# Down-projections of the first MLP: pairs of units as block multiplications with seven products

## The chip, the cores and the metric

One core of one Trainium2 chip. The kernel is written at the level of engines and semaphores: TensorE (PE; its weight loads are PEld), VectorE (DVE), ScalarE (ACT), GpSimd (POOL) and SyncE (SP), which issues nearly all transfers. The metric is the device time of one execution in microseconds, the median of the runs; before the change it is 2037.12 us (three runs, 2036.31 to 2037.77).

## The reference

32 sequences of 64 tokens with 512 features go through two layers, each an attention block with two MLPs and then an adapter. Cut to one layer:

```python
attn = softmax(einsum('btd,bTd->btT', x @ Wq, x @ Wk) * scale)
attn_out = einsum('btT,bTd->btd', attn, x @ Wv) @ Wp + bp
cms_out = gelu(attn_out @ cW1 + cb1) @ cW2 + cb2 + target_embed      # first MLP, 512 -> 2048 -> 512
modifier = gelu(concat([attn_out, cms_out]) @ mW1 + mb1) @ mW2 + mb2  # second MLP, 1024 -> 2048 -> 512
x = clip(x + cms_out + modifier, 0, 1)
h = gelu(x @ W_down[role] + b_down[role])                             # adapter, 512 -> 256 -> 512
x = layernorm(x + h @ W_up[role] + b_up[role]) * gamma[role] + beta[role]
```

All in float32.

## The kernel before

The tokens are taken in two halves of 1024, and each half goes through the two layers: four passes. Within a pass tokens form two blocks (b = 0, 1) of TB = 512. A float32 multiplication is made of three fp32r matmuls: each operand is split into a high part (ScalarE copies or applies gelu and rounds) and a low part (VectorE subtracts), and `product` (L663 to L674, the matmul on L672) issues high x high, high x low, low x high for each pair of 128x128 weights and 128x512 tokens.

**Units.** The 2048 hidden features of an MLP are taken 256 at a time: NG = 8 units for the first MLP (u = 0 to 7) and 8 for the second (u = 8 to 15). The up-projection of a unit, except of units 0 and 8 ("plain"), is a block multiplication of 2x2 blocks with seven products P1 to P7 (`term`, `terms`). A term of the first MLP has 6 matmuls, one of the second 12. The combinations of weight blocks that this needs are made by POOL in `combine` (L602), four instructions a unit; ScalarE's and VectorE's `weight_part` make the high and the low part of each. The results are put together from PSUM by ScalarE (`copy_p1`, `copy_p5`, `copy_u2`) and VectorE (`make_z22`, `make_z12`), and ScalarE's `hidden` applies gelu twice, once into a rounded high part and once into a full value, from which VectorE's `hidden` subtracts. The four 128x512 hidden blocks of a unit are H00, H10, H01, H11.

**Down-projections.** The plain form, `down` (L862), is used for units 0 to 8 and 15: for each token block and each of 4 output banks (d_out, PSUM banks 2 to 5) two hidden chunks, 6 matmuls; VectorE's `add` (L1692) then adds each bank of 128x512 to the accumulator (the result stays in SBUF). Units 9 to 14 (FAST) use a block multiplication here as well, `fast_down` (L881): seven products of two outputs each, with a part of w2 (`split_part`, `low_part`, 128x256, in one of five slots of wdp) as weights, and with hidden blocks or their differences (`hidden_sum` makes the difference, `split_sum` and `low_sum` its parts) as tokens. It works on two double banks, d_a (banks 2, 3) and d_b (4, 5); `copy_down` (L1201) copies d_a into d_b once a unit, and `fast_add` (L1673) adds a double bank, 128x1024, to the accumulator six times. POOL's `combine_down` (L618) makes the combinations of w2, four instructions of 128x256 a unit.

**Order.** Each engine runs one written-out program; nothing is scheduled at run time. PE's `mlps` (L901) puts the down-projection of unit u-1 between the terms of unit u: for units 1 to 7 the order is P1, P5, P6, block 0 of `down`, P2, P7, block 1 of `down`, P4, P3. The waits of `fast_down` that the prediction speaks of are:

```python
if i in (P6, P2):
    pe.wait_ge(d_copied, f + 1)
else:
    pe.wait_ge(acc_done, {P5: a0 - (1 if fast(u - 1) else 2), P3: a0 + 1, P1: a0 + 2, P7: a0 + 3, P4: a0 + 4}[i])
```

**Loads.** SP loads for each unit the up weights (`load_w1`, 512 KB into w1c or 1 MB into w1m) as soon as the parts of the unit before are made, and the down weights (`load_w2`, 512 KB into w2). At the start of a pass the tokens of the pass are stored to DRAM (xmid) and read back 256 KB at a time (xp) for the residual. x12 is a pair of high and low parts of one token block, which the plain units 0 and 8 read; for the first MLP it lies in the region cop, which the second MLP's operands use later.

Of the kernel before, what the change touches and what calls it, by code (L numbers as in the profile page):

```python
# [12 lines left out]
P = 128  # L13
# [59 lines left out]
DOWNS = 8 * (UNITS - len(FAST)) + 7 * len(FAST)  # L73
ADDS = 8 * (UNITS - len(FAST)) + 6 * len(FAST)
PARTS = UNITS - len(FAST) + 7 * len(FAST)

# [5 lines left out]
def cond_seq_kernel(nc, x_in, fuse_in, c1_in, c2_in, m1_in, m2_in, down_in, up_in, roles_in, rows_in, bias_in, ids_in, out):  # L82
    with ExitStack() as ctx:
# [7 lines left out]
        xmid = nc.dram_tensor("xmid", (P, NB * KC * SEQ), F32, kind="Internal").ap()  # L91
        brows = nc.dram_tensor("brows", (LAYERS, 2, BROW), F32, kind="Internal").ap()
# [6 lines left out]
        w2 = at("w2", [P, MC * V], F32, XI + 8)  # L99
        comb = at("comb", [P, 4 * P], F32, XI + 12)  # L100
        xp = at("xp", [P, TB], F32, XI + 14)
# [11 lines left out]
        aop_raw = at("aop_raw", [P, 7, 2, 2, TB], F32, AO)  # L113
        cop_raw = at("cop_raw", [P, 7, 2, 2, TB], F32, CO)
# [34 lines left out]
        wdp = at("wdp", [P, W2_SLOTS, 2, 2 * P], F32R, WT + 16)  # L149
        comb2 = at("comb2", [P, 2, 2 * P], F32, WT + 26)  # L150
# [81 lines left out]
        s_done, s_half, ss_done, mx_done, sm_ready, ex_done = (sem(n) for n in ("s_done", "s_half", "ss_done", "mx_done", "sm_ready", "ex_done"))  # L232
        rs_done, ri_done, p_zeroed, p_ready = sem("rs_done"), sem("ri_done"), sem("p_zeroed"), sem("p_ready")
# [6 lines left out]
        x12_hi, x12_lo, x12_used = sem("x12_hi"), sem("x12_lo"), sem("x12_used")  # L240
        quad_done = sem("quad_done")

        w1_loaded, w2_loaded, xp_loaded = sem("w1_loaded"), sem("w2_loaded"), sem("xp_loaded")
# [44 lines left out]
        def fasts(p, u):  # L288

            return len(FAST) * p + min(max(u - FAST[0], 0), len(FAST))  # L290

        def dn_at(p, u):

            return DOWNS * p + 8 * u - (fasts(p, u) - len(FAST) * p)

        def acc_at(p, u):

            return ADDS * p + 8 * u - 2 * (fasts(p, u) - len(FAST) * p)

        def d_at(p, u):  # L300

            return PARTS * p + u + 6 * (fasts(p, u) - len(FAST) * p)

        def plain_downs(p, u):
            return UNITS * p + u - fasts(p, u)
# [13 lines left out]
        def part_turn(u, i):  # L319
            return 7 * (u - FAST[0]) + DOWN.index(i)  # L320

        def part(u, i):
            return wdp[:, part_turn(u, i) % W2_SLOTS, :, :]

        def w2_block(half, chunk):
            return w2[:, (2 - chunk) * V + (half - 1) * 2 * P:(2 - chunk) * V + half * 2 * P]

        def part_source(i):
            return {P5: comb2[:, 0, :], P3: comb2[:, 0, :], P6: comb2[:, 1, :], P1: w2_block(1, 1), P2: w2_block(1, 2),
                    P7: w2_block(2, 1), P4: w2_block(2, 2)}[i]  # L330
# [80 lines left out]
        def h_sum(i):  # L411
            return {P5: hs_raw[:, 0, LO, 1, :], P6: zt[:, 3, :], P7: t34_raw[:, 0, LO, :], P4: t34_raw[:, 1, LO, :]}[i]
# [4 lines left out]
        def _(sp):  # L417
# [56 lines left out]
            def one_pass(half, layer, where, after):  # L474
# [37 lines left out]
                for u in range(UNITS):  # L512
# [27 lines left out]
                    if u + 1 < UNITS:  # L540
                        load_w2(u + 1)
# [1464 lines left out]
```

## Time and profile before

| | us |
|---|---|
| median of three runs | 2037.12 |
| lowest, highest | 2036.31, 2037.77 |
| the profiled execution, its own time | 2037.42 |
| its span on the core | 2035.5 |
| PE busy | 2021.2 (99%) |
| VectorE busy | 1508.2 (74%) |
| ScalarE busy | 1021.5 (50%) |
| POOL busy | 370.0 (18%) |

The granted TensorE clock over the span is 0.999 of full speed. A pass takes about 490 us; the MLPs of the first run from about 111 to 510 us. Times of an instruction in the rows are its start and its length. Instructions of one engine overlap at their ends, so a sum over many of them goes by the distance of their starts. Rows of a timeline merge neighbours of one kind and give their number (x6). A "[0.74 <-PE ...]" behind a row is the idle time of the engine before it and what ended it.

### The profile page before, as it was taken

What the parts mean: (1) busy time and instruction counts of PE and PEld (TensorE: products, weight loads), DVE (VectorE), ACT (ScalarE), POOL (GpSimd) and SP (SyncE); (2) the same over time, 40 slices, a digit from 0 to 9 for tenths busy, and PEclk for the clock granted to TensorE, in tenths of its full rate; (3) what the DMA queues carried; (4) which work ended last, traced back from release to release, by engine and by line L of the source; (5) the groups of instructions that cost most, each with busy time, mean ns of one, the idle gap of its engine ahead of it and who ended that gap; (6) DMA issues with size and microseconds to landing.
All of it is one profiled execution on the core that took longest, in us unless ns stands there. A gap on an engine that the chain in (4) does not pass through costs nothing.

```text
span 2035.5 us, 27682 instructions
## 1 busy us (share of the span) xinstructions
PE 2021.2 (99%) x9500; PEld 1692.2 (83%) x9500; DVE 1508.2 (74%) x2321; ACT 1021.5 (50%) x1844; POOL 370.0 (18%) x415
## 2 busy tenths in 40 slices
PE   9999999999999999999999999999999999999998
PEld 7888888888888888888888888888888888888887
DVE  7576677888767667888867666888886766778887
ACT  5464454555356444555435444555544544445552
POOL 0011112321101102232110110223210111032321
PEclk9999999999999999999999999999999999999999
DMA  8411211213411111112460121122252021211143
GB/s 292 166 32 42 73 47 63 73 59 113 161 68 42 52 65 60 48 62 73 155 234 22 51 63 67 37 73 73 71 189 104 11 62 42 78 62 47 62 145 95
DMA packets 42377, 169.78 MB, mean 83 GB/s; under 512 B 5624, under 2 KB 9720, under 8 KB 34808
## 3 DMA queue, kind: packets, MB, share of 16 engines
q1 hardware_dynamic: 42096, 167.97, 23.8%
q8 instruction: 80, 1.31, 0.3%
q14 instruction: 57, 0.47, 0.1%
q10 hardware_dynamic: 144, 0.03, 0.0%
HBM read 146.97 MB, written 21.01 MB: 83 GB/s over the span
## 4 chain that ended last, share of the span: by engine, by line
PE 95%; DMA 2%; DVE 2%; SPq 0%; issue 0%; POOL 0%; ACT 0%; DVEq 0%; ACTq 0%
PE psum L672 88%; DMA gains<-roles_in 1%; PE psum L966 1%; PE psum L1003 1%; PE psum L747 1%; PE psum L769 1%; DVE yt L1908 0%; PE psum L770 0%; PE psum L749 0%; SPq L422 0%; DMA fraw<-fuse_in 0%; PE psum L979 0%; PE psum L991 0%; DVE stats L1889 0%; PE psum L1015 0%
## 5 line engine op out<-in xcount | busy, mean ns | idle before, releaser
L672 PE MATMUL psum<-hs,wd 128*128 128x512 f32 x1920 | 448.8, 389 | 0.5
L672 PEld LDWEIGHTS psum<-hs,wd 128*128 128x128 f32 x1920 | 360.1, 188 | 76.9 <-DVE acc L1703 2.2
L672 PE MATMUL psum<-cop,wsm 128*128 128x512 f32 x1416 | 354.7, 389 | 0.0
L672 PE MATMUL psum<-aop,wsm 128*128 128x512 f32 x1320 | 333.0, 389 | 0.0
L672 PEld LDWEIGHTS psum<-cop,wsm 128*128 128x128 f32 x1416 | 265.8, 188 | 55.2
L672 PE MATMUL psum<-aop,wsc 128*128 128x512 f32 x1320 | 311.3, 389 | 0.0
L672 PEld LDWEIGHTS psum<-aop,wsm 128*128 128x128 f32 x1320 | 247.8, 188 | 51.4
L672 PEld LDWEIGHTS psum<-aop,wsc 128*128 128x128 f32 x1320 | 247.5, 188 | 51.4
L1679 DVE TENSOR_TENSOR acc<-psum,acc 128x1024 f32<-128x1024 f32 x144 | 175.6, 1219 | 87.2 <-PE psum L672 87.1
L1703 DVE TENSOR_TENSOR acc<-psum,acc 128x512 f32<-128x512 f32 x256 | 167.9, 684 | 84.5 <-PE psum L672 84.4
L1430 DVE TENSOR_TENSOR hs<-hs_raw,hs 128x512 fp32r<-128x512 f32 x256 | 178.8, 706 | 43.5 <-ACT hs_raw L1243 43.5
L1242 ACT ACTIVATE hs<-psum,bias 128x512 fp32r<-128x512 f32 x120 | 82.1, 684 | 237.2 <-PE psum L672 237.1
L672 PE MATMUL psum<-hs,wdp 128*128 128x512 f32 x576 | 146.2, 389 | 0.0
L1242 ACT ACTIVATE hs<-zt,bias 128x512 fp32r<-128x512 f32 x112 | 81.0, 723 | 113.7 <-PE psum L672 71.7
L672 PEld LDWEIGHTS psum<-hs,wdp 128*128 128x128 f32 x576 | 108.1, 188 | 22.4
L1171 ACT ACTIVATE wsm<-w1m 128x512 fp32r<-128x512 f32 x156 | 96.1, 622 | 37.0 <-DMA w1m<-m_in 37.0
L1430 DVE TENSOR_TENSOR wsm<-w1m,wsm 128x512 fp32r<-128x512 f32 x156 | 110.3, 723 | 1.3 <-ACT wsm L1171 1.0
L672 PE MATMUL psum<-t,wdp 128*128 128x512 f32 x432 | 109.6, 389 | 0.0
L1685 DVE TENSOR_TENSOR zt<-psum,zt 128x512 f32<-128x512 f32 x56 | 38.7, 691 | 80.2 <-PE psum L672 80.2
L609 POOL TENSOR_TENSOR comb<-w1c 128x256 f32<-128x256 f32 x28 | 20.7, 738 | 416.2 <-DMA w1c<-c_in 416.2
L672 PEld LDWEIGHTS psum<-t,wdp 128*128 128x128 f32 x432 | 81.1, 188 | 16.8
L616 POOL TENSOR_TENSOR w1m<-w1m,comb 128x512 f32<-128x512 f32 x28 | 45.4, 1620 | 269.8 <-DVE wsm L1430 269.8
(193 smaller groups left out, 3072.9 us busy)
## 6 DMA issues: line engine op xcount, KB each, us to landing
w1m<-m_in SPq DMA_DIRECT2D x32, 1024.0 KB, 4.9
w1c<-c_in SPq DMA_DIRECT2D x32, 512.0 KB, 3.5
w<-c_in SPq DMA_DIRECT2D x32, 512.0 KB, 3.6
w<-m_in SPq DMA_DIRECT2D x32, 512.0 KB, 3.5
gains<-roles_in SPq DMA_DIRECT2D x30, 512.0 KB, 5.1
fw<-fused SPq DMA_DIRECT2D x6, 2048.0 KB, 10.3
fused<-fw SPq DMA_DIRECT2D x4, 2048.0 KB, 7.6
xmid<-x SPq DMA_DIRECT2D x4, 2048.0 KB, 6.8
```

The costliest lines, as they stand in the source:

```text
L609: nc.gpsimd.tensor_tensor(st, w_block(u, 1, 0), w_block(u, 1, 1), ALU.add).then_inc(w1_sums, 1)
L616: nc.gpsimd.tensor_tensor(w_block(u, 0, 1), w_block(u, 0, 1), st, ALU.subtract).then_inc(w1_sums, 1)
L672: mm = nc.tensor.matmul(out, lhs(a), rhs(b), start=(start and n == 0), stop=(stop and n == total - 1), skip_group_check=reopened)
L747: nc.tensor.matmul(out, tq[:, j // 2, HI, j % 2, i * P:(i + 1) * P], xs[:, :, j, tile], start=(j == 0), stop=False)
L769: nc.tensor.matmul(out, val[:, HI, v_cols], val[:, :, p_cols], start=True, stop=False)
L966: nc.tensor.matmul(out, tokens, wdn_flat[:, bass.ds(role * (2 * KC * BN) + (c * KC + k) * BN, BN)], start=(b == 0 and k == 0 and a == c), ...
L1171: nc.scalar.activation(slot(u, i)[:, HI, :], w_source(u, i), ACT.Copy).then_inc(s_hi[i], 1)
L1242: nc.scalar.activation(hs[:, b, HI, m, :], h_source(h, u), ACT.Gelu, bias=b1)
L1430: return nc.vector.tensor_tensor(out, a, hi.bitcast(F32), ALU.subtract)
L1679: nc.vector.tensor_tensor(dst, bank, dst, ALU.add).then_inc(acc_done, 1)
L1685: nc.vector.tensor_tensor(zt[:, 2, :], bank_b()[:, :], zt[:, 2, :], ALU.add).then_inc(z22_done, 1)
L1703: nc.vector.tensor_tensor(dst, d_out[o][:, :], dst, ALU.add).then_inc(acc_done, 1)
```

## The change

The down-projections of units 1 to 6 (PAIRED) are no longer plain. Two units at a time, (1, 2), (3, 4) and (5, 6), go through `fast_down`: each of the seven products sums over both units in PSUM, so that a pair has seven products of 12 matmuls, six adds of 128x1024 and one copy of d_a into d_b. P5, P3 and P1 are issued within the unit behind the pair and P6, P2, P7, P4 in the one behind that; for (5, 6) all are within unit 7. Units 1 and 2 each take one token block of unit 0's plain down-projection. Unit 7 stays plain.

- The parts of w2 of a pair (14) go through seven slots, wdc; there are two buffers for w2 (w2 and w2b, the second for odd paired units).
- The hidden blocks and sums of units 1, 2, 4 and 5 go to two new sets of places, pairs, over the region cop. x12 of the first MLP is therefore stored to DRAM (kept, 1 MB) at unit 1 and read back before unit 8's third quarter product.
- POOL makes eight combinations of 128x256 for each pair, those of (1, 2) behind unit 1's `combine`, the others within `combine` of units 5 and 7, ahead of its last instruction.
- ScalarE's and VectorE's orders for units 1 to 7 are written out anew, instruction by instruction.
- The waits of several semaphores of the softmax are put on one semaphore (soft_step), with the same instructions.

PE's order and waits:

```diff
+                    for v in us:
+                        pe.wait_ge(d_lo, part_at(p, v, i))
+                        if i in SPLIT:
+                            pe.wait_ge(ht_lo, 4 * so_far(DENSE, p, v) + SPLIT.index(i) + 1)
...
+                    if i in (P6, P2):
+                        pe.wait_ge(d_copied, so_far(COPIES, p, us[-1]) + 1)
                     else:
+                        pe.wait_ge(acc_done, {P5: a0 - (2 if behind(u) is None else 1), P3: a0 + 1, P1: a0 + 2, P7: a0 + 3, P4: a0 + down_turn(u, P7)}[i])
                     out = d_b if i in (P6, P7, P4) else d_a
                     first = i in (P5, P1)
                     for o in range(2):
+                        mm = product(out[:, o, :], [(lambda a, v=v: part(v, i)[:, a, o * P:(o + 1) * P],
+                                                     lambda c, v=v: h_operand(v, i, c), None) for v in us], first, True, not first)
                     mm.then_inc(dn_done, 1)
...
+                    if u in (1, 2):
+                        terms(p, u, P1, P5, P6)
+                        down(p, 0, u - 1, 0, 1)
+                        terms(p, u, P2, P7)
+                        down(p, 0, u - 1, 2, 3)
+                        terms(p, u, P4, P3)
+                    elif u in (3, 5):
+                        terms(p, u, P1, P5, P6, P2)
+                        fast_down(p, u - 1, P5)
+                        terms(p, u, P7)
+                        fast_down(p, u - 1, P3)
+                        terms(p, u, P4)
+                        fast_down(p, u - 1, P1)
+                        terms(p, u, P3)
+                    elif u in (4, 6):
+                        terms(p, u, P1, P5)
+                        fast_down(p, u - 2, P6)
+                        terms(p, u, P6)
+                        fast_down(p, u - 2, P2)
+                        terms(p, u, P2)
+                        fast_down(p, u - 2, P7)
+                        terms(p, u, P7)
+                        fast_down(p, u - 2, P4)
+                        terms(p, u, P4, P3)
+                    elif u == NG - 1:
+                        terms(p, u, P1, P5, P6)
+                        fast_down(p, u - 1, P5)
+                        terms(p, u, P2)
+                        fast_down(p, u - 1, P3)
+                        terms(p, u, P7)
+                        fast_down(p, u - 1, P1)
+                        terms(p, u, P4)
+                        fast_down(p, u - 1, P6, P2, P7)
+                        terms(p, u, P3)
+                        fast_down(p, u - 1, P4)
```

SP's loop, POOL's order and unit 8's weights on ScalarE:

```diff
+                            for i in range(7):
+                                sp.wait_ge(s_lo[i], units(p, u, i) + 1)
+                        if u + 1 == NG:
+                            sp.wait_ge(d_lo, d_at(p, u))
+                            load_w2(u)
                         load_w1(u + 1)
...
+                    if paired(u):
+                        if u in (4, 6):
+                            sp.wait_ge(d_lo, d_at(p, u - 1))
+                            for v in group(u):
+                                load_w2(v)
+                    elif u == 0:
+                        sp.wait_ge(d_lo, d_at(p, u + 1))
+                        load_w2(2)
+                        sp.wait_ge(x12_lo, 2 * p + 1)
+                        sp.dma_start(kept, x12_flat).then_inc(x12_stored, 16)
...
+                        if u == NG - 1:
+                            sp.wait_ge(dn_done, dn_at(p, u))
+                            sp.wait_ge(x12_stored, 16 * (p + 1))
+                            sp.dma_start(x12_flat, kept).then_inc(x12_back, 16)
...
+                        elif u in (5, 7):
+                            combine_first(p, u)
+                            pair_first(p, u - 1)
+                            combine_last(p, u)
+                            pair_last(p, u - 1)
...
                 if u == NG:
+                    act.wait_ge(dn_done, dn_at(p, NG - 2) + down_turn(NG - 2, {P6: P2, P7: P7, P2: P4, P4: P4}[i]) + 1)
```

VectorE's new list where the first pair is worked off (within units 3 and 4; the lists of ScalarE and of the other units are of the same kind):

```diff
+                hidden(p, 2, H00)
+                fast_add(p, 2, P5)
+                low_part(p, 1, P1)
+                low_part(p, 2, P1)
+                low_sum(p, 2, P7)
+                make_z22(p, 3)
+                hidden(p, 2, H11)
+                fast_add(p, 2, P3)
+                low_sum(p, 2, P6)
+                low_part(p, 1, P6)
...
+                hidden_sum(p, 3, P4)
+                low_sum(p, 3, P5)
+                fast_add(p, 2, P6)
+                low_sum(p, 3, P7)
+                low_part(p, 2, P7)
+                fast_add(p, 2, P2)
+                low_part(p, 1, P4)
+                low_part(p, 2, P4)
+                weight_part(p, 5, P5)
+                fast_add(p, 2, P7)
```

## Rows read from the trace of the kernel before

**Rows 1.** The page: busy time of the engines, and the chain that ended last.
```profile
PE 2021.2 (99%) x9500; PEld 1692.2 (83%) x9500; DVE 1508.2 (74%) x2321; ACT 1021.5 (50%) x1844; POOL 370.0 (18%) x415
...
PE 95%; DMA 2%; DVE 2%; SPq 0%; issue 0%; POOL 0%; ACT 0%; DVEq 0%; ACTq 0%
```

**Rows 2.** A unit of each MLP: length, busy PE, PEld, DVE, ACT, POOL; PEclk; DMA.
```profile
166.63:187.03 20.40, 20.40 (x91) 16.90 (x90) 13.07 (x23) 9.83 (x20) 3.06 (x4) 1.00 0.17 52
358.39:386.95 28.56, 28.56 (x127) 23.66 (x126) 23.59 (x35) 15.62 (x29) 8.44 (x8) 1.00 0.18 65
```

**Rows 3.** Waits of the weight loads behind VectorE's adds, whole span.
```profile
PEld psum L672 <- DVE acc L1703: 2.2, 4, 0.5
```

**Rows 4.** Timeline of PE over one unit of the first MLP.
```profile
187.03 5.60 PE L672 MATMUL psum<-hs,wd 128*128 128x512 f32 x24
192.47 2.88 PE L672 MATMUL psum<-aop,wsc 128*128 128x512 f32 x12
...
200.63 6.96 PE L672 MATMUL psum<-aop,wsc 128*128 128x512 f32 x30
207.43 5.60 PE L672 MATMUL psum<-hs,wd 128*128 128x512 f32 x24
```

**Rows 5.** Timeline of VectorE, back-to-back instructions of three sizes.
```profile
347.78 1.22 DVE L1679 TENSOR_TENSOR acc<-psum,acc 128x1024 f32<-128x1024 f32 x1 [0.74 <-PE psum L672]
348.92 0.68 DVE L1430 TENSOR_TENSOR wsm<-w1m,wsm 128x512 fp32r<-128x512 f32 x1
349.52 0.42 DVE L1430 TENSOR_TENSOR wdp<-comb,wdp 128x256 fp32r<-128x256 f32 x1
349.86 0.68 DVE L1430 TENSOR_TENSOR wsm<-comb,wsm 128x512 fp32r<-128x512 f32 x1
```

**Rows 6.** Timeline, second MLP: products between fast_down products, and an add.
```profile
333.91 1.52 PE L672 MATMUL psum<-hs,wdp 128*128 128x512 f32 x6
336.44 1.21 DVE L1679 TENSOR_TENSOR acc<-psum,acc 128x1024 f32<-128x1024 f32 x1
336.63 1.52 PE L672 MATMUL psum<-cop,wsm 128*128 128x512 f32 x6
337.77 1.32 PEld L672 LDWEIGHTS psum<-hs,wdp 128*128 128x128 f32 x6
337.99 1.52 PE L672 MATMUL psum<-hs,wdp 128*128 128x512 f32 x6
...
346.15 1.52 PE L672 MATMUL psum<-t,wdp 128*128 128x512 f32 x6
```

**Rows 7.** Timeline, end of the second MLP: an add and the load behind it.
```profile
503.45 2.49 DVE L1703 TENSOR_TENSOR acc<-psum,acc 128x512 f32<-128x512 f32 x4
504.20 5.35 PEld L672 LDWEIGHTS psum<-hs,wd 128*128 128x128 f32 x24 [0.55 <-DVE acc L1703]
```

**Rows 8.** Timeline of ScalarE: the copy of d_a into d_b.
```profile
339.55 1.01 ACT L1205 ACTIVATE psum<-psum 128x1024 f32<-128x1024 f32 x1 [0.24 <-PE psum L672]
```

**Rows 9.** Timeline, first MLP: the chain of a combined weight part; POOL's instructions.
```profile
177.03 0.85 POOL L613 TENSOR_TENSOR comb<-comb,w1c 128x256 f32<-128x256 f32 x1 [4.37 <-DVE wsc L1430]
177.97 0.42 ACT L1171 ACTIVATE wsc<-comb 128x256 fp32r<-128x256 f32 x1 [2.15 <-issue]
178.03 0.74 POOL L616 TENSOR_TENSOR w1c<-w1c,comb 128x256 f32<-128x256 f32 x1
178.42 0.63 DVE L1430 TENSOR_TENSOR wsc<-comb,wsc 128x256 fp32r<-128x256 f32 x1 [1.13 <-ACT wsc L1171]
```

**Rows 10.** Timeline, second MLP: VectorE beside a POOL instruction.
```profile
361.93 1.68 POOL L616 TENSOR_TENSOR w1m<-w1m,comb 128x512 f32<-128x512 f32 x1 [10.01 <-DVE wsm L1430]
362.36 1.86 DVE L1430 TENSOR_TENSOR wdp<-w,wdp 128x256 fp32r<-128x256 f32 x2
```

**Rows 11.** Transfers: KB each, median us from issue to landing.
```profile
w1m<-m_in SPq DMA_DIRECT2D x32, 1024.0 KB, 4.9
w<-c_in SPq DMA_DIRECT2D x32, 512.0 KB, 3.6
```

More of the change, by code:

```diff
@@ new lines, in part_at, with w2_block, w2_odd, w2_here @@
+        def part_at(p, u, i):
+            if paired(u):
+                return d_at(p, group(u)[1]) + 2 * down_turn(u, i) + (u % 2 == 0) + 1
+            return d_at(p, u) + down_turn(u, i) + 1
+        def w2_block(u, half, chunk):
+            return (w2b if w2_odd(u) else w2)[:, (2 - chunk) * V + (half - 1) * 2 * P:(2 - chunk) * V + half * 2 * P]
+        def w2_odd(u):
+            return paired(u) and u % 2 == 1
+        def w2_here(p, u):
+            loads = [v for v in range(u + 1) if w2_odd(v) == w2_odd(u)]
+            per_pass = sum(w2_odd(v) == w2_odd(u) for v in range(UNITS))
+            return w2b_loaded if w2_odd(u) else w2_loaded, 16 * (per_pass * p + len(loads))
@@ new lines, in pair_last @@
+            def pair_last(p, u):
+                for i in (P5, P3):
+                    for v in group(u):
+                        if part_used(p, v, i):
+                            pool.wait_ge(dn_done, part_used(p, v, i))
+                        pool.wait_ge(w2_sums, w2_sum(p, v, P6))
+                        if i == P5:
+                            nc.gpsimd.tensor_tensor(part_source(v, P5), part_source(v, P6), w2_block(v, 1, 1), ALU.add).then_inc(w2_sums, 1)
+                        else:
+                            nc.gpsimd.tensor_tensor(part_source(v, P3), w2_block(v, 1, 2), part_source(v, P6), ALU.subtract).then_inc(w2_sums, 1)
@@ L790, in block_products @@
                     pe.wait_ge(s_lo[PLAIN[m, k]], n + 1)
-                    if b == 0:
+                    if kind and which == 0 and b and k == 0:
+                        pe.wait_ge(x12_back, 16 * (p + 1))
+                    elif b == 0:
                         pe.wait_ge(op_lo[(P1, P2)[k]], 2 * p + which + 1)
@@ L866, in down @@
                         pe.wait_ge(acc_done, acc_at(p, u) + o + 1)
-                    elif fast(u - 1):
+                    elif behind(u) is not None:
                         pe.wait_ge(acc_done, acc_at(p, u) - (o < 2))
@@ L896, in fast_down @@
                     for o in range(2):
-                        mm = product(out[:, o, :], [(lambda a: part(u, i)[:, a, o * P:(o + 1) * P], lambda c: h_operand(i, c), None)],
-                                     first, True, not first)
+                        mm = product(out[:, o, :], [(lambda a, v=v: part(v, i)[:, a, o * P:(o + 1) * P],
+                                                     lambda c, v=v: h_operand(v, i, c), None) for v in us], first, True, not first)
                     mm.then_inc(dn_done, 1)
@@ L922, in mlps @@
                         terms(p, u, P2)
[L923 to L929 removed]
+                        down(p, u - 1, 1, 0, 1)
+                        terms(p, u, P7)
+                        down(p, u - 1, 1, 2, 3)
                         terms(p, u, P4, P3)
```

681 lines of the change are left out of this document (536 added, 145 removed).

## Prediction

> **What bounds the kernel.** I read the page first: PE is busy 99% of the span, and the chain that ended last is 95% PE, 88% of it on L672, the line through which every product goes; VectorE is next with 74% [rows 1]. Then the two stages of one pass: in the steady units of the first MLP and of the second, PE is busy for the whole of each stretch, 20.40 of 20.40 us and 28.56 of 28.56 us, at a granted clock of 1.00, while VectorE has 13.07 and 23.59 us and ScalarE 9.83 and 15.62 us [rows 2]. The list of waits of the weight loads has almost nothing: 2.2 us behind accumulator adds in 2035 us [rows 3]. So inside the MLPs the time is the number of matmuls times their pitch, and nothing else is late. The pitch: from 187.03 to 207.43 us PE issues one unit, 24+12+24+30 = 90 matmuls (the row left out is the second block's 24), in 20.40 us [rows 4], 0.2267 us each.
>
> **What is removed.** A plain down-projection is 8 outputs x 2 chunks x 3 products of parts = 48 matmuls a unit, 96 for two. A pair needs 7 products x 2 outputs x 2 units x 3 = 84. Three pairs a pass save 36, four passes 144: 144 x 0.2267 = **-32.6 us**, all of it on the path, if PE stays fed. The units become uneven: units 1 and 2 have 66 matmuls (15.0 us), 3 and 5 have 78 (17.7), 4 and 6 have 90 (20.4), 7 has 126 (28.6).
>
> **What VectorE gains.** Pitches of back-to-back instructions, from one stretch [rows 5]: 128x1024 add 347.78 to 348.92, 1.14 us; 128x512 0.60; 128x256 0.34. Per two units, before: 14 weight parts, 28 of 128x512 (16 adds, 4 z sums, 8 hidden parts) and 2 of 128x1024 come to 4.8+16.8+2.3 = 23.9 of 40.8 us. After: 28 of 128x256 (14 weight parts, 14 low parts), 26 of 128x512 (4 z, 6 hidden, 8 sums, 8 low sums) and 6 adds of 128x1024: 9.5+15.6+6.8 = 31.9 of 38.1 us. So VectorE goes from 59% to 84% by pitch, and stays under PE. I walked its new list between successive make_z12, which can't run before a unit's last product: 13.6 us of work for the 15.0 of unit 2, 15.7 of 17.7, 16.3 of 20.4, 13.5 of 17.7, 20.7 of 20.4, 19.8 of 28.6. Only unit 6 is full, and it follows on one with 4 us to spare. ScalarE adds 14 weight splits, 8 sum splits and a 1 us copy per pair and loses 2 gelus and 2 wide copies, by my count some 26 of 38.1 us; it has 9.83 of 20.40 now [rows 2]. I take the bulk of both as hidden behind PE.
>
> **What comes onto the path: short windows.** In a pair, P3 accumulates in the banks of P5 after those were read out, P1 overwrites them after the next add, and P4 accumulates after the add of P7 (the acc_done waits in fast_down). In the second MLP two products of the next unit, 12 matmuls or 2.72 us, stand between, as between those at 333.91 and 337.99, three times 1.36 us apart [rows 6]; there an add that started late, 336.44, was done at 337.65 for a weight load at 337.77 [rows 6]. In the first MLP a term has one half only: 6 matmuls, 1.36 us. An add starts 0.27 us after the next product's first matmul (the product at 346.15 is followed at 347.51, and its add starts at 347.78 [rows 5, 6]), takes 1.22 us, and a waiting weight load begins 0.06 us behind its end (four adds take 2.49 us at a pitch of 0.60, so one is 0.69 long: 503.45+0.69 = 504.14, then 504.20 [rows 7]). Without a wait the load leads its matmul by 0.22 us (337.77, 337.99 [rows 6]). So PE loses 0.27+1.22+0.06-(1.36-0.22) = 0.41 us at each such place. These are P5 to P3, P3 to P1 and P7 to P4 in each of three pairs: 9 x 0.41 = 3.7 us a pass. In unit 7 also P1 to P6, where ScalarE's copy of 1.01 us with 0.24 before it [rows 8] gives 0.24+1.01+0.06-1.14 = 0.17. Per place the bounds are 0 (completion seen earlier than the row tells) and 1.0 (VectorE busy with one more 128x512 instruction, 0.60, when the add could start); I take 0.41, since at the places I followed VectorE has all earlier work done some us before.
>
> **Smaller terms.** Unit 2's P6 weights hang on a chain that starts only with unit 1's last gelu: VectorE sum, weight part P5, POOL 0.85, ScalarE 0.42, VectorE 0.63 [rows 9]. From the gelu's start at 13.8 us of unit 1 I get 17.7 against a load due at 17.5: 0.2 us a pass, bounds 0 and 1. Units 3 to 7 get these parts earlier.
> POOL has 8 more instructions of 128x256 per pair, 0.74 us each [rows 9], and those for pairs 3/4 and 5/6 stand ahead of combine_last, so of the P3 weights of units 5 and 7: in unit 7 P3 comes next to last, 25 us in; covered. While POOL runs, VectorE instructions that read SBUF alone wait: two of 128x256 took 1.86 us instead of 0.76, and ended 0.61 us behind POOL's 361.93+1.68 [rows 10]. A unit of the second MLP loses 23.59-21.8 (its pitches added up) = 1.8 us of VectorE to 8.44 us of POOL [rows 2]; a pair has some 12 us of POOL, so 2.5 us out of 6.2 spare. Only the burst of POOL work at the end of unit 6, where weight parts P7 and P6 of unit 7 are behind it, may show: 0 to 1.5 us a pass, I take 0.3.
> SyncE's queue: load_w1 waits for all seven parts of a unit instead of P3 alone, and P3 or P4 is made last anyway. Keeping x12 in DRAM is a 1 MB store in unit 1 and a 1 MB load in unit 7/8; w1m, of that size, lands in 4.9 us [rows 11], each has over 7 us. load_w1 of unit 8 moves behind the last part of the pair, about 19 us into unit 7; with w2 (3.6 and 4.9 us [rows 11], one after the other at worst) it is there by 28, and the first product that needs it starts at 30. The P2 and P4 weights of unit 8 wait for the last product of the pair and have the 2.72 us of the first quarter product; ScalarE 0.24+2x0.62, VectorE 0.68: 2.2 us. Covered by some 0.3 us, cost 0; if missed, under 1 us a pass.
>
> **The sum.** The profiled execution took 2037.42 us (span 2035.5, 1.9 around it), 0.3 over the median of 2037.12. Per pass stalls of 3.7+0.2+0.2+0.3 = 4.4 us, in four passes 17.6. 2037.4-32.6+17.6 = 2022.4, against the median 2022.1. **Forecast 2022 us**, 0.7% less. What a measurement can tell from no change is about 0.2%, 4 us.
>
> **Rivals.**
> A, the windows cost nothing and nothing else does: 2037.1-32.6 = 2004.5; with half the stalls 2013. For it: no add in the second MLP ever held PE up. Against: there the window is 2.72 us, here half. Chance 0.15 for 2004 to 2014.
> B, VectorE's own queue becomes late as well: besides the 0.41 each add then waits for what stands ahead of it. With 2 us more in each of pairs 3/4 and 5/6: 4 x 4 = 16 us more, 2038, with half of it 2030. For it: 84% by pitch, unit 6 at 101%. Against: 76% by pitch (21.8 of 28.56) stalls nothing in the second MLP. Chance 0.17 for 2028 to 2041.
> C, slower: POOL and VectorE serialise. From make_z12 of unit 1 to that of unit 7, VectorE has 99.6 us of work for 119.8 us of PE; POOL has 40 instructions there x 0.74 = 29.6 us. If each blocked VectorE for its whole length, VectorE would need 129.2, 9.4 us a pass over PE: 2037.1-32.6+37.6 = 2042. It decides from 20 us of blocked time a pass. For it: the stretch at 361.93 [rows 10]. Against: the second MLP would need 21.8+8.4 = 30.2 us of its 28.56 by that, and doesn't stall [rows 2, 3], since many instructions read PSUM or fall into waits. Chance 0.05.
> The Trainium skill, page "SBUF — State Buffer", section "SBUF: two separate sides", calls the port pair of VectorE and GpSimd an exclusive lock that blocks the other for the whole instruction, also for VectorE instructions with two SBUF inputs; by that rule taken for all POOL time the outcome would be C's. In the stretch above the trace agrees with it; over a unit it costs a fifth of POOL's time.
> D, the change does not do what it says: with 96 matmuls a pair nothing would go, 2037. The loops of fast_down issue 84. Chance 0.01.
> That leaves 0.62 for the forecast, 2015 to 2028.
>
> **The numbers.** Range: B's nearer part and A's half-stall case go in, 2009 to 2031; outside are A's end, most of C and the far end of B, under 0.2 together. Faster by over 0.2% (below 2033): 0.62+0.15+0.13 = 0.90; within 0.2%: 0.04; slower: 0.06.
>
> **What would show it.** Some 140 fewer PE instructions than the 9500, hs,wd down from 1920 to 768 (six units x 48 x 4 gone), PE's pitch still 0.2267. Weight loads idle behind the adds of line fast_add: 36 waits of about 0.41 us, 15 us in all, four of 0.2 behind the d_b copy. VectorE busy about 24 us more per pass in the first MLP (8.0 a pair). Second MLP unchanged at 28.56 us a unit. Wrong would be: waits of the adds over 1 us (B), no such waits (A), VectorE without idle time across units 3 to 7 with long 128x256 instructions (C), or a new wait at unit 8 behind x12_back or the P2 and P4 weights.

## The result, and the profile after

| | before | after |
|---|---|---|
| median, us | 2037.07 (8 runs) | 2030.42 (8 runs) |
| lowest, highest | 2036.31, 2038.87 | 2027.78, 2031.98 |
| the profiled execution; its span | 2037.42; 2035.5 | 2027.78; 2026.0 |

The ratio is 0.9965, with a 95% interval of 0.9954 to 0.9976: 6.65 us faster. Forecast were 2022 us, 15 us faster, with a range of 2009 to 2031 that just holds the result. The profiled execution of after happens to be the quickest of its eight; between the two profiles the gain is 9.6 us. So of the 32.6 us of matmuls taken away, 26 came back as waiting by the medians and 23 by the profiles, where 17.6 were forecast.

The page of after, its first line, the chain and two groups; it answers to [rows 1]:

```profile
PE 2004.1 (99%) x9356; PEld 1660.4 (82%) x9356; DVE 1637.2 (81%) x2513; ACT 1102.4 (54%) x2072; POOL 474.7 (23%) x511
...
PE 88%; DVE 6%; DMA 2%; issue 2%; ACT 1%; POOL 1%; SPq 0%; DVEq 0%; ACTq 0%
...
L831 PE MATMUL psum<-hs,wd 128*128 128x512 f32 x768 | 181.2, 390 | 0.5
...
L734 POOL TENSOR_TENSOR comb<-w1c 128x256 f32<-128x256 f32 x28 | 23.8, 849 | 300.4 <-DMA w1c<-c_in 300.4
```

The 144 matmuls are gone (9500 to 9356), and hs,wd fell from 1920 to 768 as the change says. PE's share still reads 99%. What is new stands in the chain: VectorE had 2% of it and has 6%, "issue" has 2%. The last line is one of POOL's old instructions, which the change does not touch: 0.74 us before, 0.85 on average now.

The stretches of after: the MLPs of the first pass, and one unit of the second MLP [rows 2]. Columns: length, busy PE, PEld, DVE, ACT, POOL, then the clock and the DMA share.

```profile
110.63:502.20 391.57, 389.13 (x1700) 317.27 (x1698) 330.37 (x481) 226.28 (x425) 109.11 (x103) 1.00 0.20 69
...
358.20:386.76 28.56, 28.56 (x127) 23.65 (x126) 23.59 (x35) 15.62 (x29) 8.43 (x8) 1.00 0.20 65
```

and the same stretch of the kernel before in its first pass:

```profile
110.69:504.20 393.51, 393.39 (x1737) 325.46 (x1735) 298.57 (x433) 206.00 (x368) 82.05 (x79) 1.00 0.19 65
```

The pass gained 1.94 us where 36 matmuls of 0.2267 are worth 8.16, so 6.2 came back as waiting. The second MLP is as it was, 28.56 us a unit and no wait at unit 8, and the clock is 1.00. All that came back lies in units 1 to 7 of the first MLP. POOL is busy 27.1 us more a pass for 24 new instructions (17.8 us at 0.74 each), VectorE 31.8 more where I had forecast 24.

The waits of the weight loads in after, whole span:

```profile
PEld psum L831 <- issue: 19.8, 45, 1.0
PEld psum L831 <- DVE wsc L1787: 10.2, 16, 1.0
PEld psum L831 <- DVE wdc L1787: 5.2, 8, 1.1
...
PEld psum L831 <- DVE acc L2063: 2.2, 4, 0.5
```

Against [rows 3], where only the last of these stood with 2.2 us, there are three new ones. The timeline of PEld over units 1 to 7 of the first pass says where they are; these are its rows with a wait, less eight more windows like the one at 163.03, of 0.44 to 0.51, and one wait of 0.17 at 236.97. The other three passes have the same waits at the same places, to about 0.1 us; only the one at 205.98 is missing in the second pass.

```profile
130.62 1.23 PEld L831 LDWEIGHTS psum<-aop,wsc 128*128 128x128 f32 x6 [1.04 <-DVE wsc L1787]
138.97 1.23 PEld L831 LDWEIGHTS psum<-aop,wsc 128*128 128x128 f32 x6 [0.31 <-DVE wsc L1787]
140.95 1.23 PEld L831 LDWEIGHTS psum<-aop,wsc 128*128 128x128 f32 x6 [0.76 <-DVE wsc L1787]
163.03 2.59 PEld L831 LDWEIGHTS psum<-pairs,wdc 128*128 128x128 f32 x12 [0.44 <-issue]
...
198.64 0.53 PEld L831 LDWEIGHTS psum<-hs,wdc 128*128 128x128 f32 x3 [1.13 <-DVE wdc L1787]
...
205.98 1.22 PEld L831 LDWEIGHTS psum<-aop,wsc 128*128 128x128 f32 x6 [0.38 <-issue]
...
235.58 1.23 PEld L831 LDWEIGHTS psum<-aop,wsc 128*128 128x128 f32 x6 [0.53 <-DVE wsc L1787]
...
249.88 0.53 PEld L831 LDWEIGHTS psum<-pairs,wdc 128*128 128x128 f32 x3 [0.22 <-issue]
```

Read them in three kinds. **The windows**: nine of 0.44 to 0.51, all at the places named in the prediction. **The copy site**: 249.88, 0.22. **The rest**: P7 of unit 1 (1.04), P5 and P6 of unit 2 (0.31, 0.76), P5 of pair 3/4 (1.13), P4 of unit 5 (0.38), P6 of unit 7 (0.53), P5 of pair 5/6 (0.17), together 4.3 us of waits a pass. For that third kind I had forecast 0.5.

A window is labelled "issue", which names nobody; the timeline of after around the first of them shows who ends it:

```profile
161.49 1.52 PE L831 MATMUL psum<-aop,wsc 128*128 128x512 f32 x6
163.06 2.98 PE L831 MATMUL psum<-pairs,wdc 128*128 128x512 f32 x12
165.88 1.52 PE L831 MATMUL psum<-aop,wsc 128*128 128x512 f32 x6
...
161.69 1.23 DVE L2039 TENSOR_TENSOR acc<-psum,acc 128x1024 f32<-128x1024 f32 x1 [1.16 <-PE psum L831]
```

The add starts 0.20 us behind the next product's first matmul, ends at 162.92, and the load follows at 163.03. VectorE stood idle 1.16 us before it, so nothing but the width of the window holds PE up. The loss is smaller than the wait. The load that waited leads its matmul by 0.03 us (163.03, 163.06) where 0.22 is usual [rows 6], so the matmul comes only 0.21 late (161.49+1.36 = 162.85 would be in time); the twelve matmuls from there take 2.82 us instead of 2.72. From 161.49 to 165.88 PE took 4.39 us for 18 matmuls, which are 4.08 at the pitch: 0.31 a window. At a wait of the third kind it is alike: around the one of 1.04, from the product at 128.49 to the one at 132.12, PE took 3.63 us for 12 matmuls, which are 2.72, so it lost 0.91.

The third kind has another face. VectorE and POOL in after, ahead of the wait at 198.64 (VectorE's rows first):

```profile
174.07 0.68 DVE L2050 TENSOR_TENSOR zt<-psum,zt 128x512 f32<-128x512 f32 x1
...
188.36 1.23 DVE L1787 TENSOR_TENSOR hs<-hs_raw,hs 128x512 fp32r<-128x512 f32 x1
189.51 1.83 DVE L1787 TENSOR_TENSOR wsc<-w1c,wsc 128x256 fp32r<-128x256 f32 x2
191.27 0.41 DVE L1787 TENSOR_TENSOR wsc<-comb,wsc 128x256 fp32r<-128x256 f32 x1
...
191.94 1.82 DVE L2023 TENSOR_TENSOR pairs_raw<-pairs_raw 128x512 f32<-128x512 f32 x2
193.87 1.04 DVE L1787 TENSOR_TENSOR pairs<-pairs_raw,pairs 128x512 fp32r<-128x512 f32 x1
194.83 1.23 DVE L2023 TENSOR_TENSOR pairs_raw<-pairs_raw 128x512 f32<-128x512 f32 x1
195.98 0.68 DVE L2050 TENSOR_TENSOR zt<-psum,zt 128x512 f32<-128x512 f32 x1
...
196.91 1.21 DVE L2039 TENSOR_TENSOR acc<-psum,acc 128x1024 f32<-128x1024 f32 x1
198.05 0.41 DVE L1787 TENSOR_TENSOR wdc<-wdc_raw,wdc 128x256 fp32r<-128x256 f32 x1
...
193.17 1.19 POOL L777 TENSOR_TENSOR wdc_raw<-comb2p,w2b 128x256 f32<-128x256 f32 x1
...
195.47 1.18 POOL L779 TENSOR_TENSOR wdc_raw<-w2b,comb2p 128x256 f32<-128x256 f32 x1
```

VectorE has no more than 0.11 us of idle time from 188.36 to the part at 198.05 for which PE waits, and many of its instructions are stretched: a 128x512 of SBUF operands takes 1.04 to 1.23 us instead of 0.68, two of 128x256 take 1.83 instead of 0.76. POOL's take 1.18 instead of 0.74. Beside each other both are slower. Where POOL stands idle, from 191.07 to 192.10, VectorE's 128x256 at 191.27 has its usual 0.41. L2050 is make_z12: of unit 3 at 174.07, of unit 4 at 195.98.

### The profile page after: what moved, and what is told of

Read it like the earlier page. It is cut to its first block, busy times and chain, and to the rows that moved or that the text cites. A ratio compares the mean times of both kernels' runs of the same rounds, so it can differ in the third digit from the quotient of the medians.

```text
span 2026.0 us, 28718 instructions
## 1 busy us (share of the span) xinstructions
PE 2004.1 (99%) x9356; PEld 1660.4 (82%) x9356; DVE 1637.2 (81%) x2513; ACT 1102.4 (54%) x2072; POOL 474.7 (23%) x511
## 4 chain that ended last, share of the span: by engine, by line
PE 88%; DVE 6%; DMA 2%; issue 2%; ACT 1%; POOL 1%; SPq 0%; DVEq 0%; ACTq 0%
PE psum L831 81%; PE psum L1161 1%; DVE wsc L1787 1%; PE psum L1198 1%; DMA gains<-roles_in 1%; PE psum L906 1%; PE psum L928 1%; DVE pairs_raw L2023 1%; DMA w1c<-c_in 1%; DVE yt L2455 0%; PE psum L1174 0%; DVE acc L2039 0%; PE psum L929 0%; PE psum L908 0%; DMA fraw<-fuse_in 0%
## 5 line engine op out<-in xcount | busy, mean ns | idle before, releaser
L2039 DVE TENSOR_TENSOR acc<-psum,acc 128x1024 f32<-128x1024 f32 x216 | 263.5, 1220 | 116.3 <-PE psum L831 115.5
L831 PE MATMUL psum<-aop,wsc 128*128 128x512 f32 x1320 | 320.7, 391 | 4.2 <-DVE wsc L1787 4.0
L831 PEld LDWEIGHTS psum<-aop,wsc 128*128 128x128 f32 x1320 | 246.0, 188 | 61.6 <-DVE wsc L1787 10.2
L831 PE MATMUL psum<-hs,wd 128*128 128x512 f32 x768 | 181.2, 390 | 0.5
L831 PE MATMUL psum<-pairs,wdc 128*128 128x512 f32 x672 | 177.6, 393 | 1.2
L831 PEld LDWEIGHTS psum<-hs,wd 128*128 128x128 f32 x768 | 143.8, 188 | 32.1 <-DVE acc L2063 2.2
L831 PEld LDWEIGHTS psum<-pairs,wdc 128*128 128x128 f32 x672 | 123.6, 188 | 36.4 <-issue 11.5
L1787 DVE TENSOR_TENSOR hs<-hs_raw,hs 128x512 fp32r<-128x512 f32 x192 | 135.5, 718 | 9.7 <-ACT hs_raw L1447 9.7
L1446 ACT ACTIVATE hs<-psum,bias 128x512 fp32r<-128x512 f32 x80 | 54.8, 685 | 76.4 <-PE psum L831 76.4
L831 PE MATMUL psum<-fw,xs 128*128 128x512 f32 x384 | 93.1, 395 | 0.0
```

The lines of the kernel that those rows point to most:

```text
L831: mm = nc.tensor.matmul(out, lhs(a), rhs(b), start=(start and n == 0), stop=(stop and n == total - 1), skip_group_check=reopened)
L1446: nc.scalar.activation(h_high(u, h), h_source(h, u), ACT.Gelu, bias=b1)
L1787: return nc.vector.tensor_tensor(out, a, hi.bitcast(F32), ALU.subtract)
L2039: nc.vector.tensor_tensor(dst, bank, dst, ALU.add).then_inc(acc_done, 1)
```

## The experiments

Two theories stood after this reading. **P**: POOL's new instructions hold VectorE up, and its lateness makes the third kind. **W**: the short windows are the larger part. Each has its own kernel. All ratios below are to the kernel before as it was measured beside each run (its medians lie from 2036.61 to 2037.48 us), with 95% intervals. That of after is 0.9954 to 0.9976; a kernel is told apart from after only where its interval lies clear of this one.

**e1_halves**: the windows. The adds of the pairs are made as two of 128x512, and P3, P1 and P4 wait for each bank by itself.

```diff
+                        if paired(u) and i in (P3, P1, P4):
+                            k = {P3: 1, P1: 2, P4: 5}[i]
+                            if o == 0:
+                                pe.wait_ge(acc_half, 18 * p + 6 * (us[-1] // 2 - 1) + k)
+                            else:
+                                pe.wait_ge(acc_done, a0 + k)
...
+                if paired(u):
+                    nc.vector.tensor_tensor(dst[:, 0, :], bank[:, 0, :], dst[:, 0, :], ALU.add).then_inc(acc_half, 1)
+                    nc.vector.tensor_tensor(dst[:, 1, :], bank[:, 1, :], dst[:, 1, :], ALU.add).then_inc(acc_done, 1)
+                    return
                 nc.vector.tensor_tensor(dst, bank, dst, ALU.add).then_inc(acc_done, 1)
```

> The changed kernel, with each of the pairs' adds of 128x1024 made as two of 128x512, and P3, P1 and P4 of a pair waiting for the add of their own bank only. Theory W (short windows): with half an add the wait for the first bank ends 0.27+0.69+0.06 = 1.02 us behind the product, before the weight load is due at 1.14, so the nine weight-load waits of 0.44 us a pass vanish and each gives back the 0.31 us that the matmuls lose now: 36 x 0.31 = 11 us, to about 2019; VectorE pays 18 x 0.06 = 1.1 us a pass. Rival L (VectorE is what is late, and the windows only show it): the same time turns up at other waits behind VectorE, gain under 3 us, 2028 to 2031.

Measured: 2027.38 us (2025.3 to 2031.1), ratio 0.9958 (0.9945 to 0.9972), span 2023.5. All nine windows are gone, but the time fell by only 3 us against after, and the two intervals overlap, so that even these 3 us are not settled. That is what rival L had said, not theory W. Its timeline of PEld and of VectorE at the place where after waited 1.13 us:

```profile
198.60 0.53 PEld L832 LDWEIGHTS psum<-hs,wdc 128*128 128x128 f32 x3 [1.98 <-DVE wdc L1794]
...
198.01 0.41 DVE L1794 TENSOR_TENSOR wdc<-wdc_raw,wdc 128x256 fp32r<-128x256 f32 x1
```

The load starts at 198.60, in after at 198.64. PE got there 0.85 us sooner and waited 0.85 us longer: here VectorE sets the time, and the three windows ahead of it were worth nothing. P4 of unit 5 went from 0.38 to 0.76 and P6 of unit 7 from 0.53 to 0.96 likewise.

**e2_thin_pool**: POOL. The 24 new instructions of POOL a pass are 16 columns wide and off the data; w2 of units 1 to 6 goes uncombined, so the sums of these units are not the reference's, and everything else is as in after.

```diff
-            if paired(u) and i in (P5, P3):
-                return wdc_raw[:, part_turn(u, i) % PAIR_SLOTS, LO, :]
+            if paired(u) and i in (P5, P3, P6):
+                return w2_block(u, *{P5: (2, 1), P3: (1, 2), P6: (2, 2)}[i])
...
-                    nc.gpsimd.tensor_tensor(w2_block(v, 2, 1), w2_block(v, 1, 1), w2_block(v, 2, 1), ALU.subtract).then_inc(w2_sums, 1)
+                    nc.gpsimd.tensor_tensor(comb2p[:, 1 - v % 2, 0:16], w2_block(v, 1, 1)[:, 0:16], w2_block(v, 2, 1)[:, 0:16], ALU.subtract).then_inc(w2_sums, 1)
```

> The changed kernel, with the 24 POOL instructions a pass that combine w2 for the pairs cut from 256 to 16 columns and taken off the data (the parts are split from uncombined w2 blocks, so the combinations of w2 of units 1 to 6 are left out); counts, waits and order are as before. Theory P (VectorE and POOL hold each other up through their shared access to SBUF): the 0.95 to 1.23 us instructions of VectorE at units 1, 4, 5 and 6 return to 0.42 and 0.68, and the waits at P7 of unit 1 (1.04), P5 of pair 3/4 (1.13), P4 of unit 5 (0.38), P6 of unit 7 and P5 of pair 5/6 (0.53+0.17) go or shrink below 0.2: about 2.5 to 3 us a pass, 2018 to 2021. Rival O (the order of the instruction lists makes them late, whatever POOL does): these waits stay within 0.2 us each, time within 3 us of the changed kernel's 2030.

Measured: 2020.21 us (2018.74 to 2021.33), ratio 0.9918 (0.9904 to 0.9931), span 2018.4: 10 us less than after by the medians, 7.6 by the spans. The waits of its weight loads, whole span, and VectorE in the stretch shown above:

```profile
PEld psum L831 <- issue: 19.8, 46, 1.0
...
PEld psum L831 <- DVE wsc L1787: 3.4, 8, 0.5
```

```profile
189.54 0.42 DVE L1787 TENSOR_TENSOR wsc<-w1c,wsc 128x256 fp32r<-128x256 f32 x1
190.89 1.49 DVE L2023 TENSOR_TENSOR pairs_raw<-pairs_raw 128x512 f32<-128x512 f32 x2 [0.94 <-ACT pairs_raw L1447]
192.48 0.69 DVE L1787 TENSOR_TENSOR pairs<-pairs_raw,pairs 128x512 fp32r<-128x512 f32 x1
```

VectorE has its usual lengths and even idles 0.94 us; P5 of pair 3/4 and P6 of unit 7 wait for nothing, of the waits behind wsc a third is left, of those behind wdc none. P4 of unit 5 waits 0.20 instead of 0.38. P7 of unit 1 still waits 0.53 and P6 of unit 2 0.32, more than theory P had left them. The windows are untouched. e2 also takes away that the parts have to wait for POOL's results; but ahead of the waits at 130.62, 198.64 and 235.58 VectorE in after runs on without idle time, so it was not waiting for a result there. P is right. W, that the windows are the larger part, is not: singly they are worth 3 us against 10.

**e6_thin_halves**: both edits together. Do they add?

> The two runs before taken together: adds of the pairs in halves, and the pairs' POOL instructions of 16 columns off the data (w2 of units 1 to 6 is not combined). Singly they gave 3 us and 10 us against the changed kernel's 2030.4. Theory S (two costs that cover each other: the waits at the windows give a late VectorE time to catch up, so taking them away pays in full only when VectorE is on time): now the windows pay their whole 36 x 0.31 = 11 us, and the time is 2020.2-11 = 2009, 21 us under the changed kernel. Rival (they add as measured singly): 2017.

Measured: 2010.87 us (2010.4 to 2012.58), ratio 0.9866 (0.9851 to 0.9881), span 2010.8. The windows are worth 9.3 us here against 3 without e2's edit, near theory S (2009) and far from its rival (2017): two losses that cover each other, since a PE that waits in a window lets a late VectorE catch up. All that waits in units 1 to 7 of its first pass now:

```profile
130.03 1.23 PEld L832 LDWEIGHTS psum<-aop,wsc 128*128 128x128 f32 x6 [0.53 <-DVE wsc L1794]
139.93 1.23 PEld L832 LDWEIGHTS psum<-aop,wsc 128*128 128x128 f32 x6 [0.48 <-DVE wsc L1794]
202.88 1.23 PEld L832 LDWEIGHTS psum<-aop,wsc 128*128 128x128 f32 x6 [0.49 <-issue]
245.13 0.53 PEld L832 LDWEIGHTS psum<-pairs,wdc 128*128 128x128 f32 x3 [0.22 <-DVE wdc L1794]
```

1.72 us a pass, 6.9 in four; by the spans 32.6-(2035.5-2010.8) = 7.9 us are still missing. The two agree within 1 us, so the matmuls are worth what was said.

**e3_units12**: only the order around units 1 and 2. POOL holds pair 1/2's combinations back until the parts of unit 1 are made and makes the last four in unit 2; the P5 part of unit 2 goes ahead of a hidden block on ScalarE and ahead of a hidden difference on VectorE.

```diff
+                            pool.wait_ge(s_lo[P7], UNITS * p + 2)
                             pair_first(p, u)
+                        elif u == 2:
+                            combine(p, u)
                             pair_last(p, u)
...
+                weight_part(p, 2, P5)
                 hidden_sum(p, 1, P5)
-                weight_part(p, 2, P5)
```

> The changed kernel, with the order alone changed at units 1 and 2: POOL waits for unit 1's P7 part before it combines w2 for pair 1/2 and does the second half of that after unit 2's combinations; ScalarE and VectorE make unit 2's P5 part before the gelu of H10 and the hidden difference. Theory: P7 of unit 1 (weight load 1.04 us late) loses 0.5 to 0.9 us less, P5 and P6 of unit 2 (0.31 and 0.76) are on time: 1.6 to 1.9 us a pass, 6 to 8 us in all, 2022 to 2024. Rival: the chain only moves, P6 of unit 2 stays late by over 0.5 us, gain under 3 us.

Measured: 2035.16 us, ratio 0.9993 (0.9984 to 1.0002), 5 us slower than after. Its first waits:

```profile
129.95 1.23 PEld L834 LDWEIGHTS psum<-aop,wsc 128*128 128x128 f32 x6 [0.50 <-DVE wsc L1790]
140.33 1.22 PEld L834 LDWEIGHTS psum<-aop,wsc 128*128 128x128 f32 x6 [0.99 <-DVE wsc L1790]
159.39 2.57 PEld L834 LDWEIGHTS psum<-pairs,wdc 128*128 128x128 f32 x12 [1.46 <-issue]
```

P7 of unit 1 went from 1.04 to 0.50, as wanted; P6 of unit 2 rose from 0.76 to 0.99, and P5 of pair 1/2, which had waited for nothing, waits 1.46. Part of the waiting was moved and none of it saved: the three places have 2.95 us of waits together, after had 2.11 in this stretch. The rival had said that the chain only moves; that the kernel gets slower neither had said.

**e4_units57**: three exchanges in VectorE's list, at P5 of pair 3/4, P4 of unit 5 and P6 of unit 7.

```diff
                 low_part(p, 3, P5)
+                low_part(p, 4, P5)
                 fast_add(p, 2, P4)
-                low_part(p, 4, P5)
...
+                make_z22(p, 5)
                 low_part(p, 4, P1)
-                make_z22(p, 5)
...
+                weight_part(p, 7, P6)
                 hidden_sum(p, 6, P5)
-                weight_part(p, 7, P7)
                 hidden_sum(p, 6, P6)
-                weight_part(p, 7, P6)
                 low_sum(p, 6, P5)
                 low_part(p, 5, P5)
                 low_part(p, 6, P5)
+                weight_part(p, 7, P7)
```

> The changed kernel, with VectorE's order alone changed at three places: the P5 part of unit 4 ahead of the add of pair 1/2's P4, make_z22 of unit 5 ahead of unit 4's P1 part, and unit 7's P6 part ahead of unit 6's differences with its P7 part behind the pair's parts. Theory: the waits at P5 of pair 3/4 (1.13 us) and at P4 of unit 5 (0.38) vanish, those at unit 7 (0.53+0.17) shrink to 0.3: 1.6 to 1.9 us a pass, 6 to 8 us, 2022 to 2024. Rival (VectorE has no room there, each instruction moved up makes another late): the sum of the waits behind VectorE in units 5 to 7 stays above 1.8 us a pass, gain under 3 us.

Measured: 2033.68 us, ratio 0.9985 (0.9976 to 0.9994), 3 us slower than after by the medians.

```profile
198.09 0.53 PEld L831 LDWEIGHTS psum<-hs,wdc 128*128 128x128 f32 x3 [0.56 <-DVE wdc L1787]
202.84 0.53 PEld L831 LDWEIGHTS psum<-hs,wdc 128*128 128x128 f32 x3 [0.79 <-issue]
...
236.04 1.22 PEld L831 LDWEIGHTS psum<-aop,wsc 128*128 128x128 f32 x6 [1.41 <-issue]
```

and PE and ScalarE at the last of these places:

```profile
236.07 1.63 PE L831 MATMUL psum<-aop,wsc 128*128 128x512 f32 x6 [1.01 <-ACT psum L1408]
...
234.20 0.63 ACT L1394 ACTIVATE hs<-hs_raw 128x512 fp32r<-128x512 f32 x1 [2.19 <-DVE hs_raw L2023]
```

P5 of pair 3/4 fell from 1.13 to 0.56, the window behind it grew from 0.44 to 0.79, P4 of unit 5 stopped waiting, and P6 of unit 7 rose from 0.53 to 1.41. The third exchange was aimed at the wrong instruction. VectorE's P6 part is now done at 233.02, but PE waits there for ScalarE's copy_p1 (L1408) as well, whose copy ends at 235.93, 0.11 ahead of the load; and ScalarE had stood idle 2.19 us for VectorE's difference (L2023), which stands behind the part now and ends at 234.16. In after the difference was done at 233.70 and the copy at 235.47, next to the part's 235.51, so that moving the part alone could gain nothing. In e3 and e4 the rival was right that little is to be gained, but both kernels came out slower than after (e4 only just clear of its interval), which neither side had said.

**e7_dve_sums**, **e8_dve_sums_halves**: is it the sharing itself, or has VectorE too much to do? The 24 combinations a pass are moved from POOL to VectorE, at about the places where POOL made them (0.42 us each there); e8 has e1's halves as well.

```diff
-                            pair_first(p, u)
-                            pair_last(p, u)
...
                 make_z22(p, 4)
+                pair_sum(p, 3, P7)
+                pair_sum(p, 4, P7)
                 low_sum(p, 3, P4)
                 hidden(p, 3, H00)
+                pair_sum(p, 3, P6)
+                pair_sum(p, 4, P6)
```

> The changed kernel, complete, with the eight combinations of w2 of each pair made by VectorE instead of POOL, each of 128x256 at a pitch of 0.34 us, put into its list at units 1, 2, 4 and 6. Theory P (it is POOL's hold on VectorE's access, 0.74 us a POOL instruction, that makes VectorE late): 24 x 0.34 = 8 us more work a pass for VectorE and yet no instruction of 0.95 to 1.23 us at units 4 and 6, and the waits there shrink: 2022 to 2026. Rival (VectorE is late for its amount of work): 2.7 us more at each pair where it is behind already, 1 us or more per pass longer, 2033 or over.

> The same with the pairs' adds in halves as well. Theory S: if VectorE is on time, the windows pay nearly in full, 2013 to 2018; a complete kernel that beats the changed one by 12 us or more. Rival: no better than the run before by over 3 us.

Measured: e7 2035.08 us, ratio 0.9984 (0.9975 to 0.9993); e8 2029.19, ratio 0.9961 (0.9948 to 0.9975). For e7 the rival was right. e8 is 5.9 us faster than e7, more than its rival allowed, but far from the 2013 to 2018 of theory S, and not told apart from after. Busy time from 150 to 262 us of the first pass, in the columns of [rows 2]; after, e2 and e7 in this order, one fence each:

```profile
150.00:262.00 112.00, 110.63 (x476) 87.92 (x475) 99.32 (x166) 71.22 (x152) 32.73 (x34) 1.00 0.16 52
```

```profile
150.00:262.00 112.00, 111.49 (x482) 89.42 (x482) 95.48 (x165) 71.47 (x152) 20.64 (x34) 1.00 0.15 52
```

```profile
150.00:262.00 112.00, 109.33 (x467) 86.19 (x466) 99.64 (x180) 70.88 (x153) 17.12 (x19) 1.00 0.15 52
```

With POOL back at 17 us, VectorE is busy for as long as in after, 99.6 of 112 us, and PE is fed worse. So in this placement VectorE loses as much to its own additional instructions as to POOL's; what is short is VectorE's time in this stretch, of which e2 gave back 3.8 us (99.32 to 95.48). POOL's share is the cause in after, as e2 shows, but taking it away at the price of 14 more instructions on VectorE in these 112 us gives nothing. How much of that is the places I chose stays open: P6 of unit 7 waits 1.63 us in e7, and no other placement was tried.

**e9_halves_swap1**, **e10_halves_swap2**: e1 was the best complete version. e9 adds the first exchange of e4 to it, e10 the first two; the third, behind which e4 waited 1.41 us, is left out.

> The kernel of e1_halves (2027.4 us) with one more edit: on VectorE the low part of unit 4's P5 weights goes ahead of the last add of pair 1/2 (P4). In e1 PE waits 1.98 us a pass at P5 of pair 3/4 behind just that part. Theory S (delays of VectorE add up, and where one instruction is late for its place alone, moving it is enough): the wait falls to under 0.8 us and little grows elsewhere, 4 x 1.2 = 5 us, so 2022 to 2024, span 2018 to 2020. Rival V (VectorE has too much to do in this stretch, whatever the order): the wait turns up at the next places behind, P3 of pair 3/4 or P4 of unit 5, and the time stays at 2026 to 2029.

> As e9_halves_swap1, and unit 5's make_z22 goes ahead of the low part of unit 4's P1 weights, so that P4 of unit 5 (0.76 us of wait in e1) finds it done; P1 of the pair comes two products later. Theory S: that wait goes too, 4 x 0.5 = 2 us more than in e9, 2020 to 2022. Rival V: no better than e9, within 2 us, or worse by up to 4, with the wait at P1 of pair 3/4 or at unit 6.

Measured: e9 2024.59 us (2022.53 to 2027.18), ratio 0.9941 (0.9927 to 0.9954); e10 2024.52 (2021.3 to 2025.58), ratio 0.9937 (0.9924 to 0.9951). In e9 the wait at P5 of pair 3/4 fell from 1.98 to 0.99, and P4 of unit 5 waits 0.41 instead of 0.76; a wait of 0.33 stands at P3 of the pair behind it, and one of 0.38 at 210.37:

```profile
197.36 0.53 PEld L832 LDWEIGHTS psum<-hs,wdc 128*128 128x128 f32 x3 [0.99 <-DVE wdc L1794]
...
201.64 0.53 PEld L832 LDWEIGHTS psum<-hs,wdc 128*128 128x128 f32 x3 [0.33 <-issue]
```

The result lies just outside of what either theory had said, 2.8 us below e1, and the intervals of e1 and e9 overlap, so that this step is not settled. In e10 P4 of unit 5 no longer waits, and the wait of 0.38 at 210.37, at unit 6's P1, has become 0.68: it ends behind ScalarE's last gelu of a hidden block, so that not all of what is left is VectorE's. That the second exchange adds nothing, and that the wait turns up at unit 6, is what the rival had said. Settled is that e10 beats both kernels: its interval lies wholly below that of after (0.9954 to 0.9976). It is 12.1 us faster than before as measured beside it (2036.61) and 5 to 6 faster than after.

## Why the prediction was wrong in its size

- **What is removed**, right: 144 matmuls, the pitch as before, and e6 recovers all but 7.9 us of the 32.6.
- **Short windows**, right in mechanism and place, nine a pass, and in the wait (0.40 more than the usual 0.04 between loads, forecast 0.41). The add starts 0.20 behind the matmul, not 0.27, and the load 0.11 behind the add, not 0.06, which cancels. The term took PE's loss to be the load's wait; PE lost 0.31, because a held load starts closer ahead of its matmul: 9 x 0.31 = 2.8 us a pass against 3.7.
- **Copy site**, right: 0.22 of wait, 0.18 more than the usual 0.04; forecast 0.17.
- **Second MLP, unit 8, x12 by way of DRAM**, right: 28.56 us a unit and no wait at unit 8.
- **Smaller terms**: the step that failed. For units 2 and 7 I had taken 0.2+0.3 = 0.5 us a pass, and 4.3 us of waits stand at seven places in units 1, 2, 5 and 7. Two steps of the working made the error. The first is the sentence "While POOL runs, VectorE instructions that read SBUF alone wait", which I then spread over a pair as 2.5 us "out of 6.2 spare". An average over a pair says nothing of a burst: in the eleven microseconds before 198.05 nine POOL instructions stand beside VectorE's list, both engines stretch (1.19 for 0.74, 1.23 for 0.68), and VectorE is late by more than it had in hand just there. The working's own walk shows it: from make_z12 of unit 3 to that of unit 4 it counted 16.3 us of VectorE for 20.4 of PE, and from 174.07 to 195.98 VectorE took 21.9 us with 2.2 of them idle, so 19.7 of work. I had priced POOL at "0.74 us each" throughout, its length beside an idle VectorE. The second is the term of 0.2 for unit 2, where I followed one chain alone, that of unit 2's P6; it measured 0.76, and P5 of unit 2 and P7 of unit 1, which had no term, 0.31 and 1.04. With 12 matmuls fewer in unit 1, PE comes to P7 of unit 1 2.7 us sooner (12 x 0.2267), while ScalarE's and VectorE's work up to there is the same, and POOL's first new instruction stands beside it too (1.04 us of wait; 0.53 in e2 without POOL's share).
- **Rivals**: B, VectorE's queue late as well, had 0.17 for 2028 to 2041, and 2030.4 came out. Its number is the nearest, and by some luck: its mechanism had the adds late, but the windows kept their 0.44, and it was mostly the weight parts that PE waited for. What I held against it, that 76% by pitch stalls nothing in the second MLP, did not carry over to 84%. C's mechanism is at work, but between single instructions of a burst and not for all of POOL's time. The Trainium skill, page "SBUF — State Buffer", section "SBUF: two separate sides", calls the port pair an exclusive lock; the traces agree that the two engines hold each other up in turn, POOL too (0.74 to 1.19 us). A, windows for nothing, did not come true.
- **Adding up**, right as a sum: with 0.13 less for PE than the load waits (1.04 against 0.91), the seven waits of the third kind cost about 3.4 us a pass, and 2.8+0.1+3.4 = 6.3, against 6.2 from the profiles. What does not add up is what the repairs give back: 3 us for e1, 10 for e2 and 19.6 for both. Taking a window away in front of a late VectorE gives nothing, so the worth of one repair depends on the others.

Taken away in this order, the 26 us are by the medians: 10.2 to VectorE's lateness from POOL (after to e2), 9.3 to the windows once that is gone (e2 to e6; 3 while it is there), and 6.4 to the chains of units 1 and 2, P4 of unit 5 and the copy site, which e6 still has (2010.9 against 2037.1-32.6 = 2004.5). What shortens these last was not found.

## What to carry to other kernels

When matmuls are taken out of a kernel that PE bounds, list every place where PE now arrives earlier and ask for each who has to be ready by then; an engine's mean load (84% here) does not answer that, its busiest ten microseconds do. Price GpSimd and VectorE instructions that meet each other at their length beside each other, not alone. Where waits share a late engine, try repairs together as well as singly: two of the three exchanges of e4, which lost 3 us, stand in the fastest complete version. And ask of each wait which of its conditions comes last and which comes next: at P6 of unit 7 two engines were done within 0.04 us of each other.

## What had not been expected of the hardware

- GpSimd's 128x256 instructions of SBUF operands took 1.12 to 1.19 us while VectorE worked on SBUF operands, against 0.73 to 0.74 alone; VectorE's 128x512 took 1.04 to 1.23 against 0.68. The slowing is mutual. The starts say the same as the lengths: in after POOL's from 193.17 to 196.62 and VectorE's at 194.83 and 195.98 are 1.15 us apart, where VectorE alone has 0.60 and POOL alone 0.70 (132.95 to 133.65); taking turns throughout would be 1.30. Beside a VectorE instruction of 128x1024 (127.99) POOL's 128x256 at 128.57 took 1.72. VectorE's instructions on PSUM kept their length beside POOL (0.68 at 195.98, beside POOL's 1.18 from 195.47).
- A 16-column POOL instruction of e2 still took 0.22 to 0.74 us, and up to 1.21 (128.67, beside VectorE's 128x1024), so it does not get shorter in proportion to its columns; VectorE beside them kept nearly its usual length (0.69 at 192.48 in e2).
- A weight load that was held up starts 0.03 us ahead of its matmul instead of 0.22, and PE then loses less than the load waited: 0.31 of 0.40 us.
